# Four joins for seven, sums of quarter products in PSUM, and a reordered start and end in an FP32R transformer block

## The reference

```python
def rfs(xw):          # xw: tokens or input_weights, width 512; ab = xis, AB = exp(xis)
    dot = xw @ (ab[:, None] * proj_matrix).T
    return 1 / sqrt(512) * AB * exp(dot - 0.5 * sum(xw * xw, -1)[..., None] * ab * ab)
x = layernorm(x + rfs(x) @ rfs(input_weights).T)         # x: 4 x 2048 x 512, float32
real = x @ cos(theta + theta_noise)
imag = x @ sin(phi + phi_noise)
x = layernorm(x + sqrt(real * real + imag * imag))
```

## Time and profile before

| | us |
|---|---|
| median of 3 runs | 697.17 (696.4 to 697.36) |
| the profiled execution | 696.49 |
| its span | 694.6 |
| PE busy in the span | 680.8 (98%) |
| DVE / ACT / POOL busy | 600.3 / 460.7 / 203.1 |
| mean granted clock of PE | 0.995 of full speed |

### The profile page before, as it was taken

How to read it: one execution, slowest core, us unless ns; L and a number is a source line. 1 busy time by engine, 2 the same in 40 slices (tenths; PEclk the granted TensorE clock), 3 DMA queues, 4 the chain that set the end, 5 groups by cost and what they waited for, 6 DMA issues and landing times. The chain is left out here.

```text
span 694.6 us, 10270 instructions
## 1 busy us (share of the span) xinstructions
PE 680.8 (98%) x3010; PEld 562.1 (81%) x3010; DVE 600.3 (86%) x968; ACT 460.7 (66%) x694; POOL 203.1 (29%) x257
## 2 busy tenths in 40 slices
PE   9999999999999999999999999999999999999993
PEld 7888888878888888888888888888888888888782
DVE  5888899889898988889888888898888888887897
ACT  7777998395666748566674855757485675847256
POOL 5772304105041140503214050320405033050324
PEclk9999999999999999999999999999999999999997
DMA  8862031471826547182654708355380835535232
GB/s 309 236 137 61 16 121 62 113 205 40 215 80 147 156 112 205 31 215 87 131 171 103 214 21 220 92 123 179 92 225 15 209 108 121 181 66 132 62 90 92
DMA packets 179254, 90.23 MB, mean 130 GB/s; under 512 B 120992, under 2 KB 149664, under 8 KB 179232
## 3 DMA queue, kind: packets, MB, share of 16 engines
q1 hardware_dynamic: 177936, 87.61, 46.5%
q0 software_dynamic: 1152, 2.10, 1.8%
q10 hardware_dynamic: 144, 0.26, 0.1%
HBM read 58.46 MB, written 31.49 MB: 129 GB/s over the span
## 5 line engine op out<-in xcount | busy, mean ns | idle before, releaser
L484 POOL TENSOR_TENSOR plain_late<-plain_late 128x1024 f32<-128x1024 f32 x26 | 68.1, 2621 | 274.7 <-ACT plain_late L835 274.7
L1009 PE MATMUL token_ps<-W_hi,F_hi 128*128 128x512 f32 x256 | 99.7, 389 | 0.9 <-DVE plain_late L1622 0.9
L1011 PE MATMUL token_ps<-W_hi,F_lo 128*128 128x512 f32 x256 | 99.6, 389 | 0.0
L1010 PE MATMUL token_ps<-W_lo,F_hi 128*128 128x512 f32 x256 | 99.6, 389 | 0.0
L737 ACT ACTIVATE o_tile<-plain_late,shift,rstd 128x512 f32<-128x512 f32 x56 | 42.6, 809 | 63.3 <-POOL shift L501 54.0
L731 ACT ACTIVATE plain_late<-plain_late 128x1024 f32<-128x1024 f32 x28 | 29.7, 1062 | 74.7 <-POOL plain_late L484 73.3
L1622 DVE TENSOR_TENSOR plain_late<-token_ps,plain_late 128x512 f32<-128x512 f32 x108 | 71.5, 682 | 3.9
L835 ACT ACTIVATE plain_late<-plain_late 128x1024 f32<-128x1024 f32 x54 | 55.2, 1056 | 19.0 <-DVE plain_late L1622 18.6
L623 ACT ACTIVATE F_hi<-plain_expo,ab 128x512 fp32r<-128x512 f32 x62 | 44.6, 720 | 31.6 <-DVE plain_expo L1253 31.5
L1121 PE MATMUL token_ps<-T_hi,zT_hi 128*128 128x512 f32 x162 | 63.1, 390 | 0.4 <-DVE zT_lo L1248 0.4
L1122 PE MATMUL token_ps<-T_lo,zT_hi 128*128 128x512 f32 x162 | 63.0, 389 | 0.0
(11 more groups left out here) (309 smaller groups left out, 1767.3 us busy)
## 6 DMA issues: line engine op xcount, KB each, us to landing
x_tok<-in_x SPq DMA_DIRECT2D x16, 1024.0 KB, 6.0
out_tokens<-o_tile SPq DMA_DIRECT2D x62, 256.0 KB, 3.1
plain_xT_lo<-in_xT SPq DMA_DIRECT2D x14, 1024.0 KB, 8.8
turned_pair<-plain_late SPq DMA_DIRECT2D x104, 128.0 KB, 3.0
plain_zT_lo<-turned_pair SPq DMA_DIRECT2D x27, 256.0 KB, 2.8
plain_zT_lo<-turned_pair SPq DMA_DIRECT2D x54, 128.0 KB, 2.8
norm_bc<-token_norms SPq DMA_DIRECT2D x15, 256.0 KB, 3.1
plain_T_hi<-in_gsT SPq DMA_DIRECT2D x4, 256.0 KB, 4.3
```

The lines of the kernel that those rows point to most:

```text
L484: pool.tensor_tensor(parts[:, p, :, 0, :], parts[:, p, :, 0, :], parts[:, p, :, 1, :], ALU.add).then_inc(sum_made, 2)
L1009: nc.tensor.matmul(o, F_hi[:, c, cols], W_hi[:, c, :], start=(c == 0), stop=False)
L1010: nc.tensor.matmul(o, F_hi[:, c, cols], W_lo[:, c, :], start=False, stop=False)
L1011: return nc.tensor.matmul(o, F_lo[:, c, cols], W_hi[:, c, :], start=False, stop=(c == C - 1))
```

## The change

- **Quarter products.** M1, M6, M5 and M3 of a pair are added up in one bank by PE itself (`onto`, a product that doesn't start a new sum); M7, M2 and M4 have a bank each. So pair 0 takes the four token banks and pair 1 the projection's four (`BANKS`). The bank holds M1, then U, then W, then C12, and ACT reads it after each step: it copies M1, U and W into `parts` and squares C12 straight from the bank. DVE keeps four joins (V, C11, C22, C21). PE waits for ACT's copy before it adds the next product to that bank.
- **Order of the products.** `PAIRED_ORDER` interleaves the two pairs instead of one after the other. In ACT's step the table switch, the sums of squares, the rounding of xT and the squares stand in a new order; DVE's `pair_sum` of pair 0 comes from POOL, and `split_columns` moves behind the joins.
- **Last blocks.** The mix of block 15 is written to the projection's banks and waits for the exponents, not for joins; M3 of block 14's first pair follows the mix's first tile. The last pair's squares, sums and statistics get a new order; tile 1's mean and variance move from ACT to DVE.
- **Start.** wT is loaded from ACT's queue, xT of the first block in four chunks from SP's, ahead of xis. Chunk 0 of wT is rounded by DVE instead of ACT, with a semaphore of its own, for which PE and POOL wait.

```diff
 # SP
             for c in range(C):
                 sp.dma_start(gs_raw[:, c, :], by_chunk(gsT)[:, c, :]).then_inc(gs_loaded[c], 16)
-                sp.dma_start(z[:, c, :], by_chunk(wT)[:, c, :]).then_inc(wT_loaded[c], 16)
+            for c in range(C):
+                sp.dma_start(xT_first[:, c, :], xT_blocks[0][:, c, :]).then_inc(xT_first_loaded[c], 16)
...
-            sp.dma_start(xT_first, xT_blocks[0]).then_inc(xT_loaded, 16)
 # POOL
-                pool.wait_ge(wT_hi_made, c + 1)
+                pool.wait_ge(wT_hi_made if c else wT_first_hi_made, max(c, 1))
...
-                pair_sum(b, 0)
                 pair_residual2(b, 0)
 # ACT
             act.sem_inc(square_done, SQUARE_CREDIT)
+            for c in range(C):
+                act.dma_start(z[:, c, :], by_chunk(wT)[:, c, :]).then_inc(wT_loaded[c], 16)
...
-                nc.scalar.activation(turned(zT_hi, c), z[:, c, :], ACT.Copy).then_inc(wT_hi_made, 1)
+                if c:
+                    nc.scalar.activation(turned(zT_hi, c), z[:, c, :], ACT.Copy).then_inc(wT_hi_made, 1)
                 square_columns(0, c, z)
...
+            def copy_U(b, p, bank, place, **how):
+                act.wait_ge(quarter_done, quarters_done(b, p, "M6", **how))
+                nc.scalar.activation(place[:, 1, 0, :], BANKS[bank]["sum"][:, :], ACT.Copy).then_inc(U_copied, 1)
+            def copy_W(b, p, bank, place, **how):
+                act.wait_ge(quarter_done, quarters_done(b, p, "M5", **how))
+                nc.scalar.activation(place[:, 1, 1, :], BANKS[bank]["sum"][:, :], ACT.Copy).then_inc(W_copied, 1)
+            def square_sum(b, p, bank, place, **how):
+                act.wait_ge(quarter_done, quarters_done(b, p, "M3", **how))
+                nc.scalar.activation(place[:, 0, 1, :], BANKS[bank]["sum"][:, :], ACT.Square).then_inc(square_done, 1)
...
+                copy_first(b, 0, 0, parts[:, 0], **how)
                 round_halves(b, 1)
                 round_half_sums(b, 1)
-                copy_first(b, 0)
-                load_table(ACT.Sqrt)
+                copy_U(b, 0, 0, parts[:, 0], **how)
             def step(b, pair, slot):
                 open_step(b)
                 act.wait_ge(x_loaded[slot], 16 * (pair + 2))
+                sum_square(b + 3, 0, slot, 1 - slot)
+                sum_square(b + 3, 1, slot, 1 - slot)
+                copy_W(b, 0, 0, first)
+                sum_square(b + 3, 2, slot, 1 - slot)
+                copy_first(b, 1, 1, second)
+                load_table(ACT.Sqrt)
+                square_second(b, 0, first)
+                square_sum(b, 0, 0, first)
+                copy_U(b, 1, 1, second)
+                square_joined(b, 0, first, "C11")
+                sum_square(b + 3, 3, slot, 1 - slot)
+                copy_W(b, 1, 1, second)
+                pair_roots(b, 0)
...
                 round_columns(0)
                 round_columns(1)
+                square_joined(b, 1, second, "C11")
+                square_sum(b, 1, 1, second)
+                square_second(b, 1, second)
 # ACT, last tiles
+                square_joined(b, 1, last_parts, "C11")
+                copy_W(b, 1, 0, last_parts, alone=True)
+                square_joined(b, 1, last_parts, "C22")
+                square_joined(b, 1, last_parts, "C21")
+                square_sum(b, 1, 0, last_parts, alone=True)
                 root_tile(1, 1, sum_made, C * b + 3)
-                square_part("C12", 0, 1)
                 root_tile(1, 0, sum_made, C * b + 4)
 # PE
                 pe.wait_ge(gs_hi_made, c + 1)
-                pe.wait_ge(wT_hi_made, c + 1)
+                pe.wait_ge(wT_hi_made if c else wT_first_hi_made, max(c, 1))
...
+                if name == "M6":
+                    pe.wait_ge(first_copied, s)
+                if name == "M5":
+                    pe.wait_ge(U_copied, s)
+                if name == "M3":
+                    pe.wait_ge(W_copied, s)
+        PAIRED_ORDER = [(0, "M1"), (0, "M7"), (0, "M2"), (0, "M6"), (0, "M4"), (0, "M5"), (1, "M1"),
+                        (0, "M3"), (1, "M7"), (1, "M6"), (1, "M2"), (1, "M5"), (1, "M4"), (1, "M3")]
...
                 for j in range(C):
-                    pe.wait_ge(joined, joins_done(e, 0, JOIN_ORDER, *BEFORE_MIX[j]))
-                    mix(b, j)
+                    pe.wait_ge(expo_made, C * (e + 2) + j + 1)
+                    mix(b, j, wide_project_ps)
+                    if j == 0:
+                        own_product(e, 0, "M3")
 # DVE
             a = squares[1]
             dve.wait_ge(squares_made, C + 2)
+            dve.wait_ge(wT_loaded[0], 16)
+            ts(turned(zT_hi, 0), z[:, 0, :], 1.0, None, ALU.mult).then_inc(wT_first_hi_made, 1)
             tt(a[0], a[0], a[1], ALU.add).then_inc(block_squares_summed, 1)
...
+                join_V(b, 0, 0, first)
+                join_C11(b, 0, 0, first)
+                join_C22(b, 0, 0, first)
+                join_C21(b, 0, 0, first)
+                join_V(b, 1, 1, second)
+                pair_sum(b, 0)
+                join_C11(b, 1, 1, second)
+                turn_norms(b + 3, 1 - slot)
+                join_C22(b, 1, 1, second)
+                join_C21(b, 1, 1, second)
                 split_columns(b + 2, 0)
                 split_columns(b + 2, 1)
-                turn_norms(b + 3, 1 - slot)
-                join_pair(b, 1)
                 pair_stats2(b, 0, 0)
```

More of the change, by code:

```diff
@@ L175, in build @@
         project_ps = [bank(f"project_ps{k}") for k in range(2)]
+        xT_first_loaded = [sem(f"xT_first_loaded_{c}") for c in range(C)]
+        wT_first_hi_made = sem("wT_first_hi_made")
         turn_ps = [bank(f"turn_ps{k}") for k in range(2)]
@@ L874, in last_steps @@
+                square_sum(b, 1, 1, second)
+                square_second(b, 1, second)
             def last_steps():
                 e, b = NB - 2, NB - 1
-                open_step(e)
-                square_tile(e, 0, 1)
-                square_tile(e, 0, 0)
+                first, second = parts[:, 0], parts[:, 1]
+                open_step(e, split=True)
+                load_table(ACT.Sqrt)
+                copy_W(e, 0, 0, first, split=True)
+                square_joined(e, 0, first, "C11")
@@ L1165, in _, with one_product @@
-            BEFORE_MIX = [("U",), ("U",), ("V",), ("W", "C22")]
-            BEFORE_PROJECT = [("C11",), ("C21",), ("C12",), ("C12",)]
+            OPENS = ["M1", "M7", "M2", "M4"]
+            def one_product(b, p, name, bank, his=pair_hi, los=pair_lo):
+                s = 2 * (b - PLAIN) + p + 1
+                if name == "M1":
+                    pe.wait_ge(halves_lo_made, s)
+                if name == "M7":
+                    pe.wait_ge(half_sums_lo_made, s)
+                if name == "M6":
[4 more added lines that the diff above has]
+                    pe.wait_ge(W_copied, s)
+                quarter_product(BANKS[bank][name if name in ("M7", "M2", "M4") else "sum"][:, :],
+                                half(p, LEFT[name], his, los), RIGHT[name], name not in OPENS)
@@ new lines, in join_C11, with join_C22 @@
+            def join_C11(b, p, bank, place, **how):
+                dve.wait_ge(first_copied, 2 * (b - PLAIN) + p + 1)
+                dve.wait_ge(quarter_done, quarters_done(b, p, "M2", **how))
+                tt(place[:, 0, 0, :], BANKS[bank]["M2"][:, :], place[:, 0, 0, :], ALU.add).then_inc(joined, 1)
+            def join_C22(b, p, bank, place):
+                dve.wait_ge(W_copied, 2 * (b - PLAIN) + p + 1)
+                tt(place[:, 1, 1, :], BANKS[bank]["M7"][:, :], place[:, 1, 1, :], ALU.add).then_inc(joined, 1)
@@ L1668, in open_step, with join_C21 @@
+            def join_C21(b, p, bank, place, **how):
+                dve.wait_ge(joined, joins_done(b, p, "V"))
+                dve.wait_ge(quarter_done, quarters_done(b, p, "M4", **how))
+                tt(place[:, 1, 0, :], BANKS[bank]["M4"][:, :], place[:, 1, 0, :], ALU.add).then_inc(joined, 1)
             def open_step(b, pair, slot, behind_plain=False):
@@ L1720, in open_step, with step @@
                 next_exponent(b, slot, 3, wide_project_ps)
+            def step(b, pair, slot, behind_plain=False):
+                first, second = parts[:, 0], parts[:, 1]
+                open_step(b, pair, slot, behind_plain)
                 landed_half_sums(b, 1)
```

350 lines of the change are left out of this document (136 added, 214 removed).

## The result

The changed kernel takes 711.56 us (median of 6 runs, 710.20 to 715.07) against 696.78 (median of 6) of the kernel before: 1.0218 times, 95% interval 1.0195 to 1.0242, so 14.8 us slower. Forecast were 706.5 and a range of 702.5 to 711.5, which the median passes by 0.06: the sign was right, the size too small by 5.1. The profiled execution is the longest of the six (715.07, span 713.3). A second profile of the same kernel, taken later, is of an execution of 708.95 (span 707.0).

A forecast was written before the change was run, and what follows sets the result against it. PE, busy 98%, was taken as the bound. Start +10.3, clock +1.7, blocks +0.3, last mix -0.8 and tail -1.8 sum to +9.7 on the profiled 696.49: 706.2, or 706.5 with half the median's 0.7 added; range 702.5 to 711.5.

The forecast's parts named there:

- The start: Head of the kernel: PE's first real matmul at 16.0 instead of 5.08, +10.9, less a wait of 0.61: +10.3 us.
- the clock: Behind PE's late start: PE restarts at 1.2 GHz after idling, costing 0 to 3.4 us, middle taken: +1.7.
- the 7 us: After PE's restart: at most the first 7 us run at half rate, upper bound 3.4 us lost.
- The blocks: Quarter-product blocks: a loop block costs nothing as it stands; with DVE later, two lie near the limit: +0.3, bounds 0 and 4.
- The account of the copy: Blocks, where one product lies between: ACT's copy and PE's wait behind it take 0.92 of 1.36 us, 0.44 to spare.
- the 0.29: Block from 347.86: copy of U of pair 0 is due at 353.49; the rounding ahead of it ended at 353.20.
- the 1.05: Each next block: DVE, its turned squares too, comes 1.05 us later, its splits running beside POOL's residual addition.
- Rival (2): Blocks: ACT's copies hold PE up in each block, 0.7 a block, +9 over 13 blocks, 715; chance 0.09.
- The last mix: Last mix: its wait of 1.15 goes, copy of U of pair 0 about 0.3 late net: -0.8, from -1.2 to +0.3.
- about when they were: Products after the last mix: the last block's halves are split at about the old time, copies having 0.44 to spare.
- the price of such a meeting: DVE's split beside POOL's addition in the earlier trace: 2.06 us against 1.22 in the mean; used for the loop blocks.
- The tail: After the last matmul: ACT squares M3's sum from PSUM, last square at 684.4 for 686.26: -1.8, bounds 0 and -2.5.

The follow-up runs named there:

- experiment 1: Changed kernel with DVE's cast of wT's chunk 0 first in DVE's queue: 699.51 us, 1.0037 times the kernel before.
- experiment 3: Changed kernel with the start undone (ACT rounds all chunks of wT, loads as before): 699.32 us, 1.0036 times the kernel before.
- 11.6 (2): Kernel before with only the changed start (loads, ACT's first loop, DVE's cast): 708.73 us, 1.0171 times the kernel before, +11.6.
- experiment 6: Kernel of experiment 3 with ACT's copies of U and, in the last blocks, W ahead of the roundings: 702.52 us, 1.0086 times the kernel before.
- experiment 7: Kernel of experiment 3 with POOL's sum and residual of block 14's pair 1 on DVE: 697.25 us, 1.0010 times the kernel before.
- 9: Kernel of experiment 7 with copy of U ahead of the rounding and DVE's feature splits ahead of the half sums: 696.66 us, 0.9999 times the kernel before.
- 10: Kernel of 9 with M2 of pair 0 ahead of M7 and the last pair's copy of U ahead of the second root: 696.26 us, 0.9993.
- experiment 4: Changed kernel with 34 warm-up matmuls for 9: 712.02 us, interval against the kernel before 1.0203 to 1.0237.
- 6 to 10: Includes one run not named singly: the edits of experiment 6 and experiment 7 together on the kernel of experiment 3, 701.31 us, 1.0070.

## Why the prediction was right on the sign and short on the size

**The start and the clock: right.** +10.3 and +1.7, together 12.0, against 12.05 (experiment 1), 12.2 (3) and 11.6 (2). PE's start at 16.0 was 16.75 and 16.24; the clock's middle value, 1.7, stands against 2.4 and 1.5. That it came so near is luck in part: no row gave the 7 us with which the prediction bounded the half rate, and the runs showed 5.0 and 3.3 us of it. Nor is the price at the median read: the two profiled executions list a mean granted clock of 0.987 and 0.989, but four of the six timed ones 0.995 or 0.996, like the kernel before; of these no profile is kept, and at the head of an execution that figure is no sure reading (last section). The restart at half rate, that no row of before showed, is now shown, and the Trainium skill's sentence in TensorE: Matmul & The Clock Gate, Part 1 (the slow clock is the default, activity releases it) agrees with the 0.50 up to 21 and the 1.00 from 22.

**The blocks: the mechanism right, the size in part.** The account of the copy (0.92 of 1.36) and the 0.29 by which the copy of U is free named the place where PE then waited, behind the rounding that waits for a landing. Mis-sized was the lateness: +0.3 was forecast, 0.6 and 3.3 were read, with bounds of 0 and 4. In the mean the 1.05 by which it let DVE and the turned squares come later was right: over the eleven loop blocks the landed squares of pair 1 are taken up 1.9 us after the block's first product in the kernel before, 3.2 and 2.9 in the two profiles after (which edit does it wasn't run). What it missed is the one block, with 5.5 and 4.0 (in the first profile DVE waited 4.03 for the landing, had 1.74 and 2.39). Why that block's landing is later than its neighbours' isn't settled. Rival (2), 0.7 in every block, didn't come true: most blocks have no gap. How near it stood, experiment 6 shows: one rounding moved, and most blocks lose 0.44.

**The last mix: the step that failed.** Forecast -0.8, read +2.9 and +1.7. The wait for the join did go, 1.15, and the copy of U in block 14 came 0.8 and 0.65 late where 0.3 was taken. What failed is the sentence behind it, that the halves of the last block are split "about when they were". In the kernel before, POOL's sum of that pair began at 670.27, 13.5 ahead of the last matmul's end (683.77), and met only one split. With four joins for seven, and with ACT's squares now ahead of its rounding, the squares are done sooner; which of the two weighs more wasn't run. POOL's sum at 686.33 stands 17.8 ahead of the last matmul's end (704.16), 1.6 of it the two gaps in between. That is just when those half sums land: POOL's sum holds DVE's 256-column sum, and POOL's residual then the 768-column split. PE lost 1.6 to it in the first profile, 2.1 in the second. The prediction knew the price of such a meeting (2.06 for 1.22 in the earlier trace rows) and used it for the loop, but didn't ask what POOL, set free earlier, would now meet at the end. Experiment 7 shows it: 2.1 us return when POOL's two instructions are taken away. The Trainium skill (SBUF — State Buffer, Who interferes with whom) calls the port pair that DVE shares with GpSimd an exclusive lock and says that issue order decides who blocks; the trace agrees with DVE's 2.63, which started behind POOL's 2.67 and ended 0.28 behind its end.

**The tail: right.** -1.8 forecast, -1.7 read twice; the last store is issued 6.0 behind the last matmul, 5.9 were forecast.

**The sum.** The start, the clock and the tail came within 0.3 each (in the first profile the start within 0.8, the clock within 0.7). Most of the 5.1 that are missing at the median lies in the blocks and the last two blocks: by medians, experiment 3 has +2.2 for all but the start, against a forecast of -2.3, so 4.5 of the 5.1. The first profile has +6.2 in the blocks and the last two blocks, the second +2.3, against a forecast of -0.5. The range left them out because it took the blocks' bound of 4 and the start's upper bound as things that don't come together, and gave the last mix no bound above +0.3.

**What the change is worth without the start.** With the start undone and the two orders mended (9 and 10) it is level with the kernel before: 0.9999 and 0.9993. PE was 98% busy and the number of matmuls is the same. In the profile of 9 the tail is 1.5 shorter and the 1.2 ahead of the last mix is gone; against that stand 1.1 in gaps at 662.9, 666.0 and 680.1 and some tenths at the start. Its span is 0.7 shorter, and it is the fastest of its eleven runs; their median shows no gain.

## What to carry to other kernels

A cast that takes 0.43 us cost 12, because of its place: before moving work to another engine, write down all that stands ahead of it in that engine's queue, and who waits for it. When a step is taken out of a path, ask of every engine that now comes earlier, also of the one that is nearly idle, what it will run beside. And a copy that must be made between two products wants nothing ahead of it in its queue that waits for a landing. What is moved behind it to make room comes later itself, so ask which work waits for that, and whether the next copy is among it.

## What the runs showed of the hardware that was not expected

The granted clock reads 1.00 from the start in every trace, and yet the warm-up matmuls come 7 to the microsecond at 2 to 3 us and 12 at 7 to 8 (experiment 4). In experiment 3 the first four real matmuls still ran slowly, 1.96 in all against the 1.17 of the earlier trace rows:

```profile
5.04 1.96 PE L1009 MATMUL token_ps<-zT_hi,gs_hi 128*128 128x512 f32 x4
```

The list of clock levels in that trace begins only at 6.76, just where the matmuls' starts go from 0.43 us apart to 0.23; in all traces it begins between 4.3 and 7.2. So at the head of an execution the rate of the matmuls tells more than that column. The same start differs between executions: with an early start (before, and experiments 1, 3 and 6 to 10) the first four took 1.17 to 2.04.

An addition of 128x1024 takes 2.4 us on POOL and 1.2 on DVE; beside it, DVE's own additions take up to 2.6 in place of 0.4. So DVE, with 2.4 us of POOL's work on top, was through sooner (experiment 7).
